# Graph attention with residual norm: value blocks in one step, paired block transposes, edges and a shorter root on POOL

## What is computed

```python
q = _split_heads(x @ Wq + bq); k = _split_heads(x @ Wk + bk); v = _split_heads(x @ Wv + bv)
scores = jnp.einsum('bhqd,bhkd->bhqk', q, k) / jnp.sqrt(32) + beta * adj[:, None]
scores = jnp.where(adj[:, None] > 0, scores, -9e15)
probs = softmax(scores, axis=-1)
out = jnp.einsum('bhqk,bhkd->bhqd', probs, v)        # heads side by side again: (B, N, D)
y = layernorm(x + out, axis=-1, eps=1e-5)            # no scale, no shift
```

## Time and profile before

| what | value |
|---|---|
| median of three runs | 624.77 us |
| profiled execution | 624.5 us, span 622.6 us, mean granted TensorE clock 0.989 |
| PE | 601.6 us busy (97%) |
| DVE | 591.8 us busy (95%) |
| ACT | 576.8 us busy (93%) |
| POOL | 400.9 us busy (64%) |
| DMA | mean 189 GB/s; the shuffle is 480 copies of 160 KB |

### The profile page before, as it was taken

How to read it: one execution, slowest core, us unless ns; L and a number is a source line. 1 busy time by engine, 2 the same in 40 slices (tenths; PEclk the granted TensorE clock), 3 DMA queues, 4 the chain that set the end, 5 groups by cost and what they waited for, 6 DMA issues and landing times. The chain is left out here.

```text
span 622.6 us, 20663 instructions
## 1 busy us (share of the span) xinstructions
PE 601.6 (97%) x6080; PEld 488.0 (78%) x6080; DVE 591.8 (95%) x2266; ACT 576.8 (93%) x2063; POOL 400.9 (64%) x639
## 2 busy tenths in 40 slices
PE   7899999999999999999999999999999999999991
PEld 6887878787878888787878787888878787878850
DVE  4989999999999999999999999999999999999885
ACT  4899999999999999999999999999999999999981
POOL 1333327667767766776766776776677676677664
PEclk8999999999999999999999999999999999999996
DMA  6248889988889988889998888998888998887832
GB/s 197 83 107 193 182 170 227 188 200 203 197 201 203 223 184 205 199 202 195 222 195 196 198 202 197 205 222 183 203 203 200 196 222 189 203 202 174 192 92 103
DMA packets 68223, 117.63 MB, mean 189 GB/s; under 512 B 10512, under 2 KB 36368, under 8 KB 68112
## 3 DMA queue, kind: packets, MB, share of 16 engines
q1 hardware_dynamic: 67024, 116.10, 81.2%
q10 hardware_dynamic: 1088, 0.20, 0.2%
HBM read 22.94 MB, written 12.58 MB: 57 GB/s over the span
## 5 line engine op out<-in xcount | busy, mean ns | idle before, releaser
L513 ACT ACTIVATE probs<-neg_scores,neg_max 128x256 f32<-128x256 f32 x768 | 382.2, 503 | 5.0 <-DVE neg_max L595 1.4
L595 DVE CUSTOM_DVE_ANT_0 neg_scores<-s_bank,bias_sb 128x256 f32<-128x256 f32 x768 | 279.7, 415 | 9.7 <-PE s_bank L458 7.7
L630 DVE STREAM_TRANSPOSE blocks<-probs 128x512 f32<-128x512 f32 x308 | 196.7, 686 | 0.0
L513 ACT ACTIVATION_READ_ACCUMULATOR probs<-neg_scores,neg_max 128x1 f32 x768 | 149.0, 194 | 0.0
L839 POOL TENSOR_SCALAR adj_sb<-adj_sb,beta_col 128x512 f32<-128x512 f32 x31 | 62.2, 2007 | 81.4 <-DVE bias_sb L643 81.4
L458 PE MATMUL s_bank<-qk 32*128 32x256 f32 x1536 | 110.0, 400 | 2.3 <-DVE neg_max L595 1.6
L382 PE MATMUL j_bank<-xt_high,w_high 128*128 128x256 f32 x567 | 110.6, 303 | 0.4 <-DVE xt_low L611 0.3
L529 ACT ACTIVATE qk<-j_bank,qk_bias 128x256 f32<-128x256 f32 x192 | 90.0, 470 | 17.1 <-PE j_bank L382 15.3
L458 PEld LDWEIGHTS s_bank<-qk 32*128 32x128 f32 x1536 | 69.4, 184 | 42.4 <-ACT qk L529 13.2
L881 POOL TENSOR_SCALAR att<-att,rstd,shift 128x384 f32<-128x384 f32 x58 | 95.6, 1656 | 6.3 <-POOL shift L878 6.3
L411 PE MATMUL j_bank<-shuffled,v_sb 128*32 128x256 f32 x1232 | 98.1, 385 | 0.2 <-ACT blocks L525 0.2
(11 more groups left out here) (82 smaller groups left out, 864.4 us busy)
## 6 DMA issues: line engine op xcount, KB each, us to landing
shuffled<-blocks SPq DMA_DIRECT2D x480, 160.0 KB, 4.1
x_sb<-in_x_dram SPq DMA_DIRECT2D x32, 384.0 KB, 6.0
out_dram<-att SPq DMA_DIRECT2D x30, 384.0 KB, 3.6
adj_sb<-in_adj_dram SPq DMA_DIRECT2D x32, 256.0 KB, 6.1
shuffled<-blocks SPq DMA_DIRECT2D x16, 128.0 KB, 2.7
blocks<-in_L_gnn_Wq_dram SPq DMA_DIRECT2D x1, 576.0 KB, 5.7
blocks<-in_L_gnn_Wk_dram SPq DMA_DIRECT2D x1, 576.0 KB, 8.0
blocks<-in_L_gnn_Wv_dram SPq DMA_DIRECT2D x1, 576.0 KB, 5.1
```

The lines of the kernel that those rows point to most:

```text
L513: nc.scalar.activation(probs[:, (T * s + t) % (T * NX), :], neg_scores[:, (T * s + t) % (T * NH), :], ACT.Exp, bias=neg_max[:, n % 2, t, h ...
L595: nc.vector.tensor_tensor_reduce(neg_scores[:, (T * s + t) % (T * NH), :], s_bank[h % J][:, t * N:(t + 1) * N], bias_sb[:, n % 2, t, :], - ...
L630: nc.vector.transpose(blocks[:, n % 2, :, h, :, :].rearrange("p k t q -> p t k q"), probs[:, slot:slot + T, :].rearrange("p t (k q) -> p t ...
```

## The change

- The three O jobs of graph n - 2 are all issued at h = 0, ahead of the scores, instead of at h = 0, 4 and 8. The other jobs move: G to h = 2, 3, 6; Q1 to 4; V0 to 5; V1 to 7. Nothing is left at h = 8; 10 and 11 have T alone.
- Two heads are turned by one DVE instruction: pairs (0, 1) and (2, 3) behind the maxima at h = 3, (4, 5) and (6, 7) at h = 7, (8, 9) at h = 11. `turn_blocks` waits for the second head's exps. NX is 6.
- `edges` of graphs 2 and later is done by POOL inside `bias`, with a wait for the maxima of the graph that used the mask buffer before.
- POOL's norm takes the short root: the two halves go by turns, two instructions a Newton step and half instead of four for both, each with a scalar read from memory. The norm of graph n - 2 runs in graph n. POOL's order is add, residual, bias, norm.
- `v_sb` has 3 buffers instead of 4, `att` 2 instead of 3, `heads_t` 3 instead of 2.
- In the last graph the O jobs of the two graphs before are grouped, G1 of the last graph comes before the end, and the sum of the graph before is one instruction.

```diff
-    NX = 5
+    NX = 6
...
             jobs = {
-                0: (("O", 0, n - 2),),
+                0: (("O", 0, n - 2), ("O", 1, n - 2), ("O", 2, n - 2)),
                 1: (("X", 0, n + 2), ("K", 0, n + 1)),
                 2: (("G", 0, n - 2), ("Q", 0, n + 1)),
-                3: (("K", 1, n + 1),),
-                4: (("O", 1, n - 2),),
-                5: (("X", 1, n + 2), ("Q", 1, n + 1)),
-                6: (("G", 1, n - 2), ("Q", 2, n + 1)),
-                7: (("V", 0, n + 1),),
-                8: (("O", 2, n - 2),),
+                3: (("G", 1, n - 2), ("K", 1, n + 1)),
+                4: (("Q", 1, n + 1),),
+                5: (("X", 1, n + 2), ("V", 0, n + 1)),
+                6: (("G", 2, n - 2), ("Q", 2, n + 1)),
+                7: (("V", 1, n + 1),),
                 9: (("X", 2, n + 2), ("K", 2, n + 1)),
-                10: (("G", 2, n - 2),),
-                11: (("V", 1, n + 1),),
             }
         else:
             jobs = {
-                0: (("O", 0, n - 2),),
-                1: (("O", 1, n - 2),),
-                2: (("G", 0, n - 2), ("O", 2, n - 2)),
+                0: (("O", 0, n - 2), ("O", 1, n - 2), ("O", 2, n - 2)),
+                2: (("G", 0, n - 2),),
                 3: (("G", 1, n - 2),),
                 4: (("G", 2, n - 2),),
                 5: (("O", 0, n),),
-                7: (("G", 0, n), ("O", 0, n - 1)),
-                8: (("O", 1, n - 1),),
-                9: (("G", 0, n - 1), ("O", 2, n - 1)),
-                10: (("G", 1, n - 1), ("O", 1, n)),
-                11: (("G", 2, n - 1),),
+                7: (("G", 0, n),),
+                8: (("O", 0, n - 1), ("O", 1, n - 1), ("O", 2, n - 1)),
+                9: (("G", 0, n - 1), ("G", 1, n - 1), ("O", 1, n)),
+                10: (("G", 2, n - 1), ("G", 1, n)),
             }
...
             def turn_blocks(n, h):
 
-                dve.wait_ge(exp_ready, T * (H * n + h + 1))
+
+                dve.wait_ge(exp_ready, T * (H * n + h + 2))
...
-                nc.vector.transpose(blocks[:, n % 2, :, h, :, :].rearrange("p k t q -> p t k q"),
-                                    probs[:, slot:slot + T, :].rearrange("p t (k q) -> p t k q", q=HD)).then_inc(blocks_ready, 1)
+                nc.vector.transpose(blocks[:, n % 2, :, h:h + 2, :, :].rearrange("p k h t q -> p (h t) k q"),
+                                    probs[:, slot:slot + 2 * T, :].rearrange("p t (k q) -> p t k q", q=HD)).then_inc(blocks_ready, 1)
...
-
-                    if h % J == 0:
-                        turned_now = (h,)
-                    elif h % J == 3 and h < HV:
-                        turned_now = (h - 2, h - 1, h)
+                    if h % J == 3:
+                        for job in jobs_of(n, h):
+                            if job[0] == "G":
+                                take(job)
+
+                    if h % J == 3 and h < HV:
+                        turned_now = (h - 3, h - 1)
                     else:
-                        turned_now = range(2 * J + 1, HV) if h == 2 * J + 2 else ()
+                        turned_now = (2 * J,) if h == H - 1 else ()
...
-                    if h == 11 and 3 <= n < B - 1:
-                        moments(n - 3)
-                    if h == 11 and n + 2 < B:
-                        edges(n + 2)
+                    if h == 11 and 2 <= n < B - 1:
+                        moments(n - 2)
...
             def bias(n):
 
 
+                if n >= 2:
+                    pool.wait_ge(adj_in, (n + 1) * DMA)
+                    pool.wait_ge(max_ready, T * H * (n - 1))
+                    take_wait()
+                    nc.gpsimd.tensor_scalar(bias_sb[:, n % 2, :, :], adj_sb[:, :, :], 0.0, MASKED,
+                                            ALU.is_le, ALU.mult).then_inc(not_edge_ready, 1)
                 pool.wait_ge(not_edge_ready, n + 1)
...
                 for _ in range(NEWTON):
-                    link(nc.gpsimd.tensor_tensor(nt_a[:, :], rstd[:, :], rstd[:, :], ALU.mult))
-                    link(nc.gpsimd.tensor_tensor(nt_b[:, :], nt_a[:, :], var_eps[:, :], ALU.mult))
-                    link(nc.gpsimd.tensor_scalar(nt_c[:, :], nt_b[:, :], -0.5, 1.5, ALU.mult, ALU.add))
-                    link(nc.gpsimd.tensor_tensor(rstd[:, :], rstd[:, :], nt_c[:, :], ALU.mult))
...
+                    for t in range(T):
+                        linked(rstd_at[t])
+                        b_at[t] = link(nc.gpsimd.tensor_scalar(nt_b[:, t:t + 1], var_eps[:, t:t + 1], rstd[:, t:t + 1],
+                                                               rstd[:, t:t + 1], ALU.mult, ALU.mult))
+                    for t in range(T):
+                        linked(b_at[t])
+                        rstd_at[t] = link(nc.gpsimd.tensor_scalar(rstd[:, t:t + 1], nt_b[:, t:t + 1], 1.5, rstd[:, t:t + 1],
+                                                                  ALU.add, ALU.mult))
...
                 if n + 2 < B:
+                    residual(n + 2)
                     bias(n + 2)
-                if n >= 3:
-                    layer_norm(n - 3)
-                if n + 2 < B:
-                    residual(n + 2)
+                if n >= 2:
+                    layer_norm(n - 2)
             add_residual(B - 3)
-            layer_norm(B - 4)
             norm_pair()
```

More of the change, by code:

```diff
@@ L48, in graph_attention_program @@
     NP = 4
[L49 removed]
+    CHAIN = 2 * T * NEWTON + 3
     scale = float(HD) ** -0.5
@@ L168, in graph_attention_program @@
         qk = sb("qk", [P, 2, 2, G, N])
-        v_sb = sb("v_sb", [P, 4, T, D])
+        v_sb = sb("v_sb", [P, 3, T, D])
         neg_scores = sb("neg_scores", [P, T * NH, N])
@@ L177, in graph_attention_program @@
         shuffled = sb("shuffled", [P, 2, T, J, HV, T, HD])
-        heads_t = sb("heads_t", [P, 2, N])
-        att = sb("att", [P, 3, T, D])
+        heads_t = sb("heads_t", [P, 3, N])
+        att = sb("att", [P, 2, T, D])
         stats = sb("stats", [P, 2, T, 6])
@@ L208, in graph_attention_program @@
         adj_in = sem("adj_in")
-        out_done = [sem(f"out_done{n}") for n in range(3)]
+        out_done = [sem(f"out_done{n}") for n in range(2)]
         ident_zero = sem("ident_zero")
@@ L261, in att_of @@
             if n < B - 1:
-                return att[:, n % 3, :, :]
+                return att[:, n % 2, :, :]
             return shuffled[:, n % 2, :, :, :, :, :].rearrange("p k a h t q -> p (k a h t q)")[:, 0:T * D].rearrange(
@@ L316, in shuffle @@
                 heads = block_heads(n)
-                sp.wait_ge(blocks_ready, HV * n + heads)
+                sp.wait_ge(blocks_ready, (HV * n + heads) // 2)
                 if n >= 2:
@@ L326, in store @@
                 sp.wait_ge(normed, T * (n + 1))
-                sp.dma_start(out_v[n], att[:, n % 3, :, :]).then_inc(out_done[n % 3], DMA)
+                sp.dma_start(out_v[n], att[:, n % 2, :, :]).then_inc(out_done[n % 2], DMA)
             load_x(0)
@@ L360, in _ @@
             store_half(B - 2, 1)
-            for n in (B - 3, B - 2, B - 1):
-                sp.wait_ge(out_done[n % 3], DMA * (n // 3 + (T if n > B - 3 else 1)))
+            for n in (B - 2, B - 1):
+                sp.wait_ge(out_done[n % 2], DMA * (n // 2 + T))
         @block.tensor
@@ L530, in take @@
                 elif kind == "V":
-                    ins = nc.scalar.activation(v_sb[:, n % 4, a, :], b[:, 0:D], ACT.Identity)
+                    ins = nc.scalar.activation(v_sb[:, n % 3, a, :], b[:, 0:D], ACT.Identity)
                 elif kind == "X":
@@ L616, in take @@
                     if n < B - 1:
-                        wait(dve, out_done[n % 3], n // 3 * DMA)
+                        wait(dve, out_done[n % 2], n // 2 * DMA)
                     ins = nc.vector.tensor_tensor(
@@ L694, in linked @@
                     take_wait()
-                take(("G", 1, B - 1))
                 sum_with_x(B - 1, slice(0, 2 * P))
@@ L854, in add_residual @@
                 pool.wait_ge(res_ready, n + 1)
-                nc.gpsimd.tensor_tensor(att[:, n % 3, :, :], att[:, n % 3, :, :], x_sb[:, n % XB, :, :], ALU.add).then_inc(y_ready, 1)
+                nc.gpsimd.tensor_tensor(att[:, n % 2, :, :], att[:, n % 2, :, :], x_sb[:, n % XB, :, :], ALU.add).then_inc(y_ready, 1)
             def layer_norm(n):
-                step = [0]
+                step = [CHAIN * n]
                 def link(ins):
@@ L862, in link, with linked @@
                     ins.then_inc(chain, 1)
-                    pool.wait_ge(chain, CHAIN * n + step[0])
+                    return step[0]
+                def linked(count):
+                    pool.wait_ge(chain, count)
                     take_wait()
@@ L878, in layer_norm @@
-                link(nc.gpsimd.tensor_tensor(shift[:, :], mean_var[:, n % 2, :, 0], rstd[:, :], ALU.mult))
-                assert step[0] == CHAIN
+                linked(link(nc.gpsimd.tensor_scalar(var_eps[:, :], mean_var[:, n % 2, :, 1], -0.5, -0.5 * EPS, ALU.mult, ALU.add)))
```

(8 more changed lines are left out.)

42 lines of the change are left out of this document (15 added, 27 removed).

## The result

The changed kernel takes 644.72 us (median, 642.61 to 645.27) against 625.08 us for the one before in the same session: a ratio of 1.031 [1.0296, 1.0322]. The forecast was 608.5 us and faster; it is slower, by more than the gain that was expected. The profiled execution took 644.43 us, with a span of 642.5 against 622.6.

What follows compares the result with a forecast made beforehand. PE was taken as the bound at 18.38 us a graph, falling to 17.9 (shuffle loop 17.8 plus 0.1 waits). Savings of 13.4 (28 graphs), 0.4 (graph 30) and 2.4 (ends) sum to 16.2: 608.5 us, range 602 to 619.

Steps and rivals of the forecast that it cites:

- the sentence on ACT in the DVE part: exps(6) waits for pair (0, 1), about 0.5 us later; the sixth slot gives back one head, so no cost.
- The shuffle loop: First shuffle copy through landing, values, scores and back to the last turn: 35.6 us over two graphs, 17.8 a graph.
- PE's term: Values in one step save tile-shape switches, 2.55 to 1.84 us; PE falls from 18.38 to 17.7 a graph.
- The rival that the shuffle lands later still: Landing 17.1 us instead of 16.0 gives 18.35 a graph, no gain but the end: 621 us; chance 0.05.
- DVE's own work: Edges leave (0.31 us), ten transposes become five (0.4): DVE from 18.2 to 17.5 us a graph.
- POOL: Edges added (2.2 us), root chain cut from 5.8 to 4.7: POOL 17.4 us a graph (15 to 18.5).
- the rival that makes it the bound: POOL's pointer-scalar instructions don't overlap, chain 7.2 us, POOL 19.9 a graph: about 664 us; chance 0.12.
- The start: Graphs 0 and 1 have no value blocks and were given no gain.
- The end: Merged O blocks, shorter DVE tail and earlier POOL pair chain in the last graphs: 2.4 us together (0.5 to 3.5).
- Slower: Chance 0.11 that the kernel measures slower by more than 1.2 us, nearly all from the POOL rival.
- The first rival: O-O joins drain or engines hold each other up; PE needs 18.0 to 18.3 a graph: 612 to 619 us; chance 0.2.

Runs made afterwards that it cites:

- the kernel with the early landing: Changed kernel with each pair as two single turns in the same places and only 8 of 16 shuffle copies from the third graph on: 622.88 us.
- the square: Four kernels, us a graph: as changed 18.96; half the shuffle copies left out 18.96; single turns in the new places 18.79; both 18.17.
- the version that beats both: Kernel before with values in one step, edges and short root on POOL, six probability slots, single turns in their old places: 621.18 us, ratio 0.994.

## Why the prediction was wrong, point by point

**The step that failed** is the sentence on ACT in the DVE part: the later block for the exponentials "costs nothing as long as ACT (at most 17.7) has slack". Against the interval of before, 18.39, ACT (17.7 busy) had 0.6 us of slack a graph and DVE (17.6) 0.8, and both were spent, in turns, in one loop of 18.95 us: in the changed kernel DVE waits for `xt_high` 1.2 us a graph and ACT for `blocks` 1.1. I had compared the busy times of four engines, each with its own sum, and the shuffle as the one loop between engines. I had not followed the loop from a probability slot to the turn that frees it, to the maxima and `xt_low` ahead of that turn on DVE, to ACT's `xt_high`, to the exponentials ahead of it. A pair makes this loop longer twice: it can't begin before the second head is there, and it frees the first head's slot only when both are done, some 0.6 us later. The sixth slot gives room for one head; two heads are now released as one.

**The shuffle loop was sized 2 us short.** I had 35.6 for two graphs. In the kernel with single turns in the new places, where it is the loop that holds, the trace gives 37.6: first copy to first value block 16.2 (forecast 16.0), values to their scores 2.75 (2.4, a slip that PE's term below explains), scores to the next graph's first scores 12.0 (12.0), and from there to the first copy 6.6 (1.0 + 4.2 = 5.2). The last term is the large one. DVE isn't free 1.0 us after those scores start, because it is still turning the four heads of h = 7; it comes 1.65 after them, and then waits 0.5 for `xt_high`:

```profile
306.53 2.48 DVE L625 STREAM_TRANSPOSE blocks<-probs 128x512 f32<-128x512 f32 x4
308.94 0.38 DVE L589 CUSTOM_DVE_ANT_0 neg_scores<-s_bank,bias_sb 128x256 f32<-128x256 f32 x1
...
310.15 0.42 DVE L605 TENSOR_TENSOR xt_low<-j_bank,xt_high 128x256 fp32r<-128x256 f32 x1 [0.47 <-ACT xt_high L527]
```

(That is the kernel with the early landing, whose scores start at 307.29.) Half of 37.6 is 18.8, and 18.79 was measured. The rival that the shuffle lands later still had the right place and the wrong cause: the landing stayed at 16.0, and the length came from DVE's part of the loop.

**PE's term** had the right mechanism and a wrong sum. The idle ahead of the scores, 17.2 us over 26 graphs in PEld's rows, is one of 0.41 and one of 0.25 a graph, as forecast. Two value blocks in a row are free, as forecast too: the matmuls of the three blocks start in twelve groups of four, and the step is 0.215 us from one group to the next, over both joins. The row of 34 is the first eight groups and the start of the ninth, at 324.35, so 1.72 for eight:

```profile
322.63 2.14 PE L402 MATMUL j_bank<-shuffled,v_sb 128*32 128x256 f32 x34 [0.49 <-DMA shuffled<-blocks]
324.39 0.39 PE L402 MATMUL j_bank<-probs_t,v_sb 128*32 128x256 f32 x2
324.57 0.41 PE L402 MATMUL j_bank<-shuffled,v_sb 128*32 128x256 f32 x2
...
324.78 0.41 PE L402 MATMUL j_bank<-shuffled,v_sb 128*32 128x256 f32 x2
...
325.00 0.41 PE L402 MATMUL j_bank<-shuffled,v_sb 128*32 128x256 f32 x2
...
325.36 0.50 PE L449 MATMUL s_bank<-qk 32*128 32x256 f32 x4
```

By the rule cited from the Trainium skill, TensorEngine Tiling (Array Packing), Key Properties, a join within one mode costs nothing, and these rows agree. What failed is the length of a block. I had said that four groups 0.215 apart need 0.69; four times 0.215 is 0.86. PEld's rows had misled me: PE's two first groups of weights are loaded together, so four groups show three starts (324.11, 324.35, 324.57 in the earlier trace rows), while before the matmuls of that block start four times:

```profile
324.11 0.41 PE L411 MATMUL j_bank<-shuffled,v_sb 128*32 128x256 f32 x2
...
324.35 0.39 PE L411 MATMUL j_bank<-shuffled,v_sb 128*32 128x256 f32 x2
...
324.57 0.39 PE L411 MATMUL j_bank<-shuffled,v_sb 128*32 128x256 f32 x2
...
324.78 0.39 PE L411 MATMUL j_bank<-shuffled,v_sb 128*32 128x256 f32 x2
```

So of the 1.00 from a block to its scores only 0.14 was the switch, not 0.31, and saving it twice brings 0.28 us a graph instead of 0.62. The sum on the prediction's own rows is then 0.37 saved and 18.0 a graph, not 17.7; the runs give a floor of 18.17 (three blocks in 2.76 us, about 0.05 more behind the turned probabilities, and about 0.1 that I can't place). Even without both loops PE had 0.22 a graph to give, not 0.7: 6 us of the 13.4 that the steady graphs were to bring. This alone would have kept the kernel far from 608.5: the one of the square that stands at this floor takes 622.9 us with its start and its end.

**DVE's own work** came out as said: two pairs take 2.29 us from 311.95 to 314.24 against 2.41 for four singles, edges are gone, and it is busy 17.6 us a graph (17.5 forecast).

**POOL** also: the chain is 4.81 us (4.7 forecast), edges 1.94 (2.2 with its wait), and it idles 1.5 to 2.2 us a graph for the maxima or the adjacency, so the rival that makes it the bound didn't happen.

```profile
305.28 1.94 POOL L830 TENSOR_SCALAR bias_sb<-adj_sb 128x512 f32<-128x512 f32 x1 [2.17 <-DVE neg_max L586]
...
310.90 0.19 POOL L867 TENSOR_SCALAR var_eps<-mean_var 128x2 f32<-128x2 f32 x1
...
315.71 3.30 POOL L885 TENSOR_SCALAR att<-att,rstd,shift 128x384 f32<-128x384 f32 x2 [0.22 <-POOL shift L882]
```

**The start** was put at nothing and cost 4.9 us in the profiled execution. The first graph has no graph ahead that gives the shuffle time to land: PE reaches the three value blocks at once and stands still.

```profile
55.94 1.65 PEld L402 LDWEIGHTS j_bank<-shuffled,v_sb 128*32 128x32 f32 x32 [2.46 <-ACT probs_t L516]
```

In the version that beats both, the start costs 1.2 us (its fourth reciprocal at 95.22, against 94.03), no more than two executions of one start can differ by.

**The end** was put at 2.4 us less and came out even. The four intervals of the last graphs are 38.2 us against 37.0, and what follows the last reciprocal is 1.2 us shorter, so DVE's shorter tail and POOL's earlier pair chain (ACT's last norms wait for it until 636.97 of 642.5, as until 616.45 of 622.6 in the earlier trace rows) gave back what the order lost. With the last graph's order of before, the four intervals are 36.1 (the version above) against 37.6 with the new order and the same turns. From the first of them to the end it is 48.9 against 49.8 us, so 0.9 is lost in all. Those two kernels differ in the graph of the norm as well, so that the new order is what costs, and which of its merges, isn't shown.

**The chances.** Slower had 0.11, nearly all on POOL's chain. The first rival had named the right kind of cause, engines that hold each other up, and priced it at no more than PE's slack. It had no loop written out, and a loop has no such ceiling.

## What to carry to other kernels

Where several engines stand within a microsecond of each other, equal busy times don't add up to a forecast: for each buffer that goes round between two in-order engines, write the loop out (who frees the slot, what stands ahead of the freeing instruction on its engine, what that waits for) and sum it against the interval, before and after. Fusing two instructions saves their fixed share and delays the release of the first one's buffer by the second one's length: here 0.06 us gained a pair, and 0.8 us a graph lost where nothing else held (18.96 against 18.17 with the landing early), or 0.17 where the second loop stood behind (18.96 against 18.79). When undoing one suspected part changes little, a second loop may stand right behind the first: take both away together before dropping either. And count the pitch of a block on the matmuls, not on the weight loads: n groups cost n steps, and loads that run ahead show one step less.

## What the runs showed of the hardware

The granted clock fell after a short idle time of PE. In the changed kernel PE waits for the first shuffle (2.46 us ahead of 55.94 in PEld's row, 2.25 from the last matmul's end to the next); the clock is 1.00 up to 56 us, and then it is 0.80, 0.50 and 0.85 in three stretches of 2 us, 0.50 being the lower of its two levels, 1.2 GHz, and the three value blocks take 4.2 us instead of 2.8:

```profile
56.00:58.00 2.00, 2.00 (x32) 1.43 (x36) 1.14 (x2) 1.45 (x6) 0.58 (x1) 0.80 0.03 11
58.00:60.00 2.00, 2.00 (x23) 0.84 (x14) 0.00 (x0) 0.73 (x3) 1.90 (x2) 0.50 0.83 184
60.00:62.00 2.00, 2.00 (x25) 1.50 (x22) 0.31 (x1) 1.48 (x6) 1.82 (x2) 0.85 0.98 259
```

With half of the copies left out (only from the third graph on, so with nearly the same idle time, 2.24 us between matmuls) the clock stayed at 1.00 in that execution, and the blocks took 2.8 us:

```profile
58.00:60.00 2.00, 2.00 (x36) 1.16 (x28) 0.00 (x0) 1.80 (x8) 1.90 (x2) 1.00 0.73 156
```

So in two executions one gap was followed by a fall and the other wasn't; the 1.4 us that it costs is part of the 4.9 at the start. The first 20 us differ in the same way from one profiled execution to another: the clock was down for some us in nine of the eighteen and stayed at 1.00 in others, so starts of two kernels can't be compared to better than about 1.2 us.

An issue of a shuffle copy (160 KB) holds ACT for 0.82 us on average, where on SP sixteen take 10.2 to 11.2 us, 0.64 to 0.70 each, and only other transfers stand behind them: a queue on an engine with work isn't free. Value blocks in a row cost PE nothing at their joins: twelve groups 0.215 us apart. And on POOL the short instructions with a scalar read from memory, two at a time in alternation, take 0.33 and 0.26 us each (0.67 and 0.51 for two), and the whole root 4.81 us.
